# Expert products of two slots brought together on TensorE, in a transformer block with neighbourhood attention and a 16-expert layer

## The reference, cut to what matters

```python
scores = softmax(xf @ gate_w.T)                       # 4608 tokens, 16 experts
topw, topi = top_k(scores, 2)
comb = zeros(T, 16).at[arange(T)[:, None], topi].set(topw)
h = silu(einsum('td,eid->tei', xf, w1)) * einsum('td,eid->tei', xf, w3)   # 192 -> 512
h = h * comb[:, :, None]
y = einsum('tei,edi->td', h, w2)                      # 512 -> 192
z = (silu(xf @ sw1.T) * (xf @ sw3.T)) @ sw2.T         # shared expert, 1024 wide
t = t + y + z
```

## Time and profile before

| what | value |
|---|---|
| time, median of 3 runs | 1105.67 us (1105.12 to 1107.93) |
| profiled execution, its own time | 1104.32 us |
| its span in the profile | 1102.5 us |
| PE (TensorE matmuls) busy | 1051.4 us, 95% of the span |
| ACT (ScalarE) / DVE (VectorE) / POOL (GpSimd) busy | 51% / 44% / 44% |
| granted TensorE clock | 0.99 of full speed |
| L1410, L1415, L1426 (main, tail, down) on the chain that ended last | 12%, 7%, 10% of the span |

### The profile page before, as it was taken

How to read it: one execution, slowest core, us unless ns; L and a number is a source line. 1 busy time by engine, 2 the same in 40 slices (tenths; PEclk the granted TensorE clock), 3 DMA queues, 4 the chain that set the end, 5 groups by cost and what they waited for, 6 DMA issues and landing times.

```text
span 1102.5 us, 32309 instructions
## 1 busy us (share of the span) xinstructions
PE 1051.4 (95%) x12184; PEld 855.2 (78%) x12184; DVE 489.3 (44%) x1826; ACT 566.1 (51%) x1061; POOL 486.3 (44%) x746
## 2 busy tenths in 40 slices
PE   6897999999999999899999999999999999999992
PEld 4564777777777766577767777999999999999992
DVE  5764888888888736622222222222222222222220
ACT  2776888888888721111111113555555555555550
POOL 2111556565656410166654100555555555555541
PEclk9998999999999999999999999999999999999996
DMA  4654344444444432234532321233333333333325
GB/s 117 194 188 129 103 131 136 130 140 130 138 131 135 128 109 97 89 112 153 180 132 83 92 68 51 44 51 51 51 52 51 51 51 51 52 52 51 52 38 142
DMA packets 89996, 108.52 MB, mean 98 GB/s; under 512 B 12048, under 2 KB 81320, under 8 KB 89656
## 3 DMA queue, kind: packets, MB, share of 16 engines
q1 hardware_dynamic: 69528, 86.12, 24.6%
q0 software_dynamic: 19056, 20.14, 11.5%
q10 hardware_dynamic: 1264, 0.22, 0.1%
HBM read 74.58 MB, written 35.34 MB: 100 GB/s over the span
## 4 chain that ended last, share of the span: by engine, by line
PE 86%; DMA 5%; DVE 4%; ACT 2%; issue 2%; SPq 1%; POOLq 0%; DVEq 0%; ACTq 0%
PE ps L1410 12%; PE ps L1315 10%; PE ps L1235 10%; PE ps L1426 10%; PE ps L1358 8%; PE ps L1415 7%; PE ps L1221 6%; PE ps L1255 6%; PE ps L1320 5%; DMA acc_dram<-ys,lists 4%; PE ps L1266 2%; PE ps L1141 2%; PE ps L1397 1%; PE ps L1284 1%; ACT q_T L658 1%
## 5 line engine op out<-in xcount | busy, mean ns | idle before, releaser
L623 POOL DMA_INDIRECT acc_dram<-ys,lists x87 | 137.6, 1581 | 237.5 <-DVE ys L1105 217.1
L1098 DVE TENSOR_TENSOR m_h<-m_sg,ps 128x512 f32<-128x512 f32 x87 | 59.8, 688 | 287.0 <-ACT m_sg L744 287.0
L701 ACT ACTIVATE probs<-probs,nmax 128x212 f32<-128x212 f32 x432 | 168.4, 466 | 4.6 <-DVE nmax L870 4.6
L1410 PE MATMUL ps<-xa,wring 128*128 128x128 f32 x1392 | 169.7, 275 | 0.3 <-ACT xa L738 0.3
L731 ACT ACTIVATE s_sg<-ps 128x384 f32<-128x384 f32 x96 | 47.1, 491 | 237.6 <-PE ps L1315 233.1
L1410 PEld LDWEIGHTS ps<-xa,wring 128*128 128x128 f32 x1392 | 162.3, 192 | 0.5 <-issue 0.5
L1315 PE MATMUL ps<-c_x,sw13a_sb 64*128 64x384 f32 x768 | 145.1, 488 | 4.5 <-DVE s_h L1053 4.5
L870 DVE CUSTOM_DVE_ANT_0 probs<-ps,bmask 128x212 f32<-128x212 f32 x432 | 134.8, 368 | 24.0 <-PE ps L1221 23.7
L761 ACT COPY wring<-w_sb 128x1536 f32 x87 | 128.1, 1472 | 29.2 <-issue 29.2
L1426 PE MATMUL ps<-w_sb,m_h 128*128 x696 | 136.4, 339 | 0.0
L1235 PE MATMUL ps<-ident_sb,probs 128*98 128x128 f32 x864 | 118.9, 280 | 0.2
(11 more groups left out here) (141 smaller groups left out, 1334.6 us busy)
## 6 DMA issues: line engine op xcount, KB each, us to landing
vst<-v_dram SPq DMA_DIRECT2D x144, 147.0 KB
w_sb<-in_w13a SPq DMA_DIRECT2D x8, 1024.0 KB, 5.8
v_dram<-a_v SPq DMA_DIRECT2D x12, 576.0 KB, 3.3
w_sb<-in_w SPq DMA_DIRECT2D x8, 768.0 KB, 6.6
xn_dram<-xn SPq DMA_DIRECT2D x36, 128.0 KB
w_sb<-in_w13b SPq DMA_DIRECT2D x8, 512.0 KB, 7.2
a_x<-in_x SPq DMA_DIRECT2D x12, 288.0 KB, 3.9
x_p<-in_x SPq DMA_DIRECT2D x36, 96.0 KB
```

What stands on the lines that cost most here:

```text
L623: nc.gpsimd.indirect_dma_start(acc_dram, bass.IndirectOffsetOnAxis(ap=lists[:, j, 0:1], axis=0), ys[:, j % V8, :], None, compute_op=ALU.ad ...
L701: nc.scalar.activation(here, here, ACT.Exp, bias=nmax[:, batch % 2, r:r + 1], scale=-1.0).then_inc(b_exp, 1)
L1410: mm(ps[:, g + k, 128 * f:128 * (f + 1)], wring[:, j % 2, k, 128 * f:128 * (f + 1)], xa[:, j % 2, 0:128], start=f == 0, stop=False, skip_g ...
```

## The change

Slots are taken in pairs (j, j + 1), j even. The function `up` is split into `up_ready` (the waits), `up_main` and `up_tail`, each with a flag that says whether it comes first in its PSUM banks or adds to what is there. For the first slot of a pair the main products come first, for the second the tail products. TensorE's order for a pair is then: main(j), `y_mm(j-1)`, tail(j), tail(j+1), main(j+1), `x_T(j+2)`, `x_T(j+3)`, `y_mm(j)`. The same matmuls are issued as before. The last slot, 86, stands alone: main(86), `y_mm(85)`, tail(86), `y_mm(86)`. ScalarE and VectorE take their steps in an order that goes with it. Buffers, waits within the steps, GpSimd's and SyncE's programs are as before.

```diff
--- before.py
+++ after.py
@@ -767,11 +767,18 @@
             act.wait_ge(c_b, 8 * NB)
             weights_out(0)
             xT_out(0)
-            for j in range(USED):
+            xT_out(1)
+            weights_out(1)
+            for j in range(0, USED, 2):
+                d_silus(j)
+                if j + 2 < USED:
+                    weights_out(j + 2)
+                    xT_out(j + 2)
                 if j + 1 < USED:
-                    xT_out(j + 1)
-                    weights_out(j + 1)
-                d_silus(j)
+                    d_silus(j + 1)
+                if j + 3 < USED:
+                    xT_out(j + 3)
+                    weights_out(j + 3)
 
 
         @block.vector
@@ -1105,11 +1112,13 @@
                 nc.vector.tensor_scalar(ys[:, j % V8, :], ps[:, 6 + j % 2, 0:D], lists[:, j, 1:2].bitcast(f32), None,
                                         ALU.mult).then_inc(d_y, 1)
 
-            for j in range(USED):
-                h_out(j)
+            for j in range(0, USED, 2):
                 if j:
                     y_out(j - 1)
-            y_out(USED - 1)
+                h_out(j)
+                if j + 1 < USED:
+                    h_out(j + 1)
+                y_out(j)
 
 
         @block.tensor
@@ -1398,23 +1407,31 @@
                              ident_sb[:, :])
                 ins.then_inc(d_xTps, 1)
 
-            def up(j):
-                g = 2 * (j % 2)
+            def up_ready(j):
                 pe.wait_ge(d_wA, j + 1)
                 pe.wait_ge(d_xTev, j + 1)
                 if j >= 2:
                     pe.wait_ge(d_silu, j - 1)
                     pe.wait_ge(d_h, j - 1)
+
+            def up_main(j, first):
+                g = 2 * (j % 2)
                 for f in range(4):
-                    for k in range(2):
-                        mm(ps[:, g + k, 128 * f:128 * (f + 1)], wring[:, j % 2, k, 128 * f:128 * (f + 1)],
-                           xa[:, j % 2, 0:128], start=f == 0, stop=False, skip_group_check=True)
+                    for k, made in enumerate((d_a, d_b)):
+                        ins = mm(ps[:, g + k, 128 * f:128 * (f + 1)], wring[:, j % 2, k, 128 * f:128 * (f + 1)],
+                                 xa[:, j % 2, 0:128], start=first and f == 0, stop=not first, skip_group_check=True)
+                        if f == 3 and not first:
+                            ins.then_inc(made, 1)
+
+            def up_tail(j, first):
+                g = 2 * (j % 2)
                 for f in range(4):
                     for k, made in enumerate((d_a, d_b)):
                         half = slice(64 * k, 64 * (k + 1))
                         ins = mm(ps[:, g + k, 128 * f:128 * (f + 1)], wring[half, j % 2, 2, 128 * f:128 * (f + 1)],
-                                 xa[half, j % 2, 128:256], start=False, stop=True, skip_group_check=True)
-                        if f == 3:
+                                 xa[half, j % 2, 128:256], start=first and f == 0, stop=not first,
+                                 skip_group_check=True)
+                        if f == 3 and not first:
                             ins.then_inc(made, 1)
 
             def y_mm(j):
@@ -1429,16 +1446,24 @@
                 ins.then_inc(d_yps, 1)
 
             x_T(0)
-            for j in range(USED):
+            x_T(1)
+            for j in range(0, USED, 2):
+                up_ready(j)
+                up_main(j, True)
+                if j:
+                    y_mm(j - 1)
+                up_tail(j, False)
                 if j + 1 < USED:
-                    x_T(j + 1)
-                up(j)
+                    up_ready(j + 1)
+                    up_tail(j + 1, True)
+                    up_main(j + 1, False)
+                for after in (j + 2, j + 3):
+                    if after < USED:
+                        x_T(after)
                 if j == 0:
                     pe.wait_ge(d_down, 16 * EX // 2)
                     pe.wait_ge(c_z, 3 * NB)
-                else:
-                    y_mm(j - 1)
-            y_mm(USED - 1)
+                y_mm(j)
 
 
 # ---- launch: one core; inputs laid out as the program reads them ----
```

## The result

The changed kernel takes 1092.43 us in the median of 4 runs (1091.35 to 1092.64), against 1105.72 us before. The ratio is 0.9874 with an interval of 0.9857 to 0.9891, so it is 1.3% faster. The forecast was 1089.9. The direction and most of the size are right, and 2.5 of the 15.8 us are missing. The profiled execution has a span of 1089.5 us.

A forecast was written before the change was run, and what follows sets the result against it. TensorE, busy without a break, was taken to bound the kernel. The last scatter comes 16.4 us earlier, less 0.6 for stalls at `issue`: 1105.67 - 15.8 = 1089.9 us, range 1088.0 to 1097.5.

The forecast's parts named there:

- The price of a round trip: TensorE going into and out of 64-row tail products: 0.395 us each, 43 of 87 saved, 17.0 us.
- rival A: TensorE's switch between 128 and 64 rows: each saved round trip gives only 0.19 us, 8.2 us in all, 1097.5; chance 0.09.
- The entry from a down product: TensorE's way into the tail, now from a down product: first long step +0.094 us, the same as from main.
- Covers on the other engines: ScalarE and VectorE steps in a pair finish 0.8 to 2.2 us before TensorE needs them, so none is late.
- rival C: Main(j+2) waits for xa(j+2) behind a late weight copy on ScalarE: 10.7 us slower, 1116; chance 0.06.
- TensorE's gain: TensorE's time over the slots: 43 x 0.395 = 17.0 us less, a pair taking 8.793 us.
- the chain of scatters: GpSimd's scatters, each landing before the next starts: 4.35 us a slot, staying just under TensorE's pace.
- pressed scatter: A GpSimd scatter that waits for the landing of the one before it; its period was taken as 4.35 us.
- the two stalls: GpSimd's two long waits at `issue`: 1.2 and 0.8 us, of which about 0.6 us still there at the end.
- The margin: Spare time of the scatters against TensorE: 8.793 us for two slots against 8.70, 0.09 us a pair.
- Rival B: Scatters take over the pace: at 4.45 us a slot gain 9.7, 1096; at 4.50 gain 5.4, 1100; chance 0.14.

The follow-up runs named there:

- The seam: Changed kernel with the two transposes x_T(j+2) moved between tail(j) and tail(j+1), parting the 64-row products: 1103.01 us, ratio 0.9975.
- two-accumulator pair: Changed kernel and the one before, each with odd slots' scatters sent to a second accumulator, their share left out of the output: 1087.29 and 1102.73 us.
- control: Changed kernel with the same two transposes x_T(j+2) moved between main(j) and the down products of slot j-1: 1094.64 us, ratio 0.9891.
- down products moved: Kernel before with y_mm(j-1) between main(j) and tail(j), slot by slot without pairs, and y_out(j-1) ahead of h_out(j): 1100.44 us, ratio 0.9952.
- cover gone: Changed kernel with both transposes of the next pair behind y_mm(j), so nothing stands between them and main(j+2): 1112.53 us, ratio 1.0067.

## Why the prediction was right, and what it missed

- **The price of a round trip**, 0.395 us, from the long steps of the earlier trace rows: right. 8.793 us a pair was forecast, 8.792 is there. The seam shows the cause by experiment: with the same matmuls and one more round trip a pair goes back to 9.14, and with the same transposes moved elsewhere it stays at 8.79. The half price (rival A) is out: both long steps went.
- **What the Trainium skill states** ("TensorEngine Tiling (Array Packing)", Key Properties): a change of tiling mode drains the engine, a change of tile alone doesn't. The runs agree on where a price is paid: the tiles of w1 and w3 alternate at 0.112 us a pair, tail(j) to tail(j+1) costs nothing, and each change between 128 and 64 rows costs two long steps. That both steps belong to a drain is not shown.
- **The entry from a down product**: 0.094 was taken from the earlier trace rows, and the step in the pair is the same.
- **Covers on the other engines**: right, TensorE waits for nobody inside the pairs. The copy of xa was laid out to end 8.80 - 7.85 = 0.95 us ahead of its user, and 0.95 is there; its removal turned the gain into a loss. So the place that rival C names is real. It didn't occur, and its own way there, the weight copy running late, was not tried.
- **TensorE's gain.** 17.0 us went by the count, less 1.5 for the last slot, whose silu and `h_out` nothing covers. From the start of main(0) to the last `ys`, the trace has 400.15 us before and 384.48 after: 15.7 less. The two-accumulator pair has 15.4.
- **The term that was mis-sized is the chain of scatters**, and in it the landings: a slow one was put at nothing. The prediction took 4.35 us for a pressed scatter, from the earlier trace rows, which left 0.09 us a pair to catch up with, and expected 0.6 us of lateness at the end. Until slot 52 an even slot's scatter is on time, 0.81 to 0.91 us after its `ys`. By the prediction's count slot 52's starts at 920.1; it starts at 920.28. From there to the last scatter are 34 periods and 152.3 us. The count has 34 x 4.35 + 2.0 for the two stalls = 149.9. Of the 2.4 us between them 2.0 are two slow landings, 4.87 us at slot 58 and 4.21 at slot 71, where 3.56 is the median. The other 0.4 is a period of 4.36 in place of 4.35. So the last scatter starts at 1072.56 where 1070.1 was forecast.
- **The margin is as thin as was counted.** 64 of the 86 periods after are pressed. Their mean is 4.36 us without the two behind slow landings, and 4.39 with them, the half of TensorE's 8.79. Between disturbances 0.05 to 0.1 us a pair are caught up (0.09 were counted), far too little: an even slot's scatter starts 1.9 us after its `ys` at slot 54 and 1.7 at slot 58, 3.0 at slot 60 and 2.75 at slot 66, 4.2 at slot 72 and 3.9 at slot 84.
- **Rival B** was thus half right. It had the place, and a period of 4.45 was too long. At 4.39 with the slow landings in it the chain was level with TensorE, a case between forecast and rival.
- The stalls at `issue` were counted right, 1.2 and 0.8 us at the same slots. The slow landings could not be read from before: the earlier trace rows has a maximum of 3.8 us. They are no accident of one trace. Each trace of a kernel in pairs has at least two landings over 3.9 us, the control's six.

## What to carry to other kernels

Read a full engine by the distances between starts: steps that are longer than the rest at each change of kind are a price per change, and grouping the kinds saves it in full, provided the operands are ready a group earlier. Before such a gain is booked, compare the new pace with the shortest period of every serial chain beside it, by its mean with the rare slow cases in it; where the two are nearly level, a disturbance stays almost whole to the end. When a chain is pressed, look at what stands between the release and the next start: here it was the place of one wait.

## What was not expected of the hardware

- Leaving 64-row products costs less for a transpose than for a main or down product: 0.15 us instead of 0.20. The transposes' loads are shorter too, 0.14 against 0.19 us.
- A wait that stands in the indirect DMA's own instruction lets GpSimd start it 0.28 us after the release; in a separate instruction ahead of it, 0.77 to 0.84 us.
- Slow landings go with instruction fetches. In the traces of six kernels (before, after, seam, control, down products moved, cover gone) 37 scatters took over 3.9 us to land. In each case an instruction packet of 16 KB, of which there are about 31 in the stage, had started between 1.4 and 3.5 us after the scatter's start. Not each fetch in that stretch came with a slow landing, least of all those that began after 3.0 us. In the kernel before, none of its fetches began 1.4 to 3.0 us after a scatter's start, and no landing was slow; in the kernel with the cover gone there were 17. The five other traces have 14 more slow landings, each with such a fetch. One row of the changed kernel for 947.5 to 952.5 us, the window of its slowest landing (queue: packets, MB, share of the engines):

```profile
q8 instruction: 1, 0.02, 1.9%
```

That the fetch delays the landing is a reading of these coincidences. No run moved the fetches by themselves, so it stays open, as does what GpSimd does at `issue` before slots 53 and 68.
